# Set-up of a conditioned state-space block: evictions in front of normalisation, token loads from ScalarE's queue, a projection made in the first units

## What is computed

```
shift, scale, gate = split(silu(c) @ Wada.T + bada)
x1   = ln(x; norm1) * (1 + scale) + shift          # skip = x1
xn   = ln(x1; norm2)
mz   = xn @ Wz.T + bz ;  mx = silu(xn @ Wx.T + bx)
z1   = mz @ Wc1.T + bc1 ;  z2 = flip(mz @ Wc2.T + bc2)
y    = mx * (ssm1(z1) + flip(ssm2(z2)))
out  = x + gate * (y @ Wf.T + bf + skip)

ssm(u): dbc = u @ Wdbc.T ; dlt, B, C = split(dbc, [64, 16, 16])
        delta = softplus(dlt @ Wdt.T + bdt) ; A = -exp(Alog)
        h_t = exp(delta A) h_{t-1} + delta B u_t ;  y_t = C h_t + u_t Dp
```

## Time and profile before

| | us |
|---|---|
| median of three executions (3287.22 to 3289.47) | 3288.13 |
| the profiled execution | 3287.01 |
| its span in the profile | 3285.2 |
| the folds 2 to 15 with the last turn, 55.7 to 221.5 | 165.8 |
| from there to the main block, 221.5 to 234.4 | 12.9 |
| the main block, from 234.4 | 3050.8 |

### The profile page before, as it was taken

The page is one execution under the profiler, slowest core; times in us unless marked ns, Lnnn a source line. Parts: engine busy times, 40 slices in busy tenths (PEclk is TensorE's granted clock), DMA queues, the critical chain, the costliest instruction groups (busy, mean ns, idle before and its releaser), DMA issues.

```text
span 3285.2 us, 54883 instructions
## 1 busy us (share of the span) xinstructions
PE 2993.0 (91%) x19924; PEld 2375.2 (72%) x19924; DVE 3017.2 (92%) x2008; ACT 2678.5 (82%) x5151; POOL 2903.7 (88%) x1288
## 2 busy tenths in 40 slices
PE   8887999899998999899999999899998999899999
PEld 5765666677677666678877767678777666677789
DVE  2838999999999999999999999999998999999994
ACT  1448999988888999987788999987877999988772
POOL 1528999999999999999999999999998999999993
PEclk9989999999999999999999999999999999999999
DMA  5775334644476333645465334645566343645463
GB/s 224 236 244 171 136 117 137 227 154 163 162 248 207 130 123 131 228 144 163 159 243 192 130 123 134 224 139 165 165 217 207 120 132 130 232 136 163 156 198 111
DMA packets 207053, 560.40 MB, mean 171 GB/s; under 512 B 20200, under 2 KB 66472, under 8 KB 202560
## 3 DMA queue, kind: packets, MB, share of 16 engines
q1 hardware_dynamic: 203424, 538.01, 48.5%
q0 software_dynamic: 2304, 16.78, 1.3%
q10 hardware_dynamic: 1056, 2.10, 0.2%
HBM read 476.19 MB, written 80.63 MB: 169 GB/s over the span
## 4 chain that ended last, share of the span: by engine, by line
PE 49%; ACT 20%; DVE 12%; issue 10%; POOL 1%; DVEq 0%; ACTq 0%; POOLq 0%
PE y L888 14%; PE slot L899 10%; PE mb L859 9%; ACT abuf L1134 8%; PE mb L969 6%; DVE hbuf L1326 6%; ACT slot L1195 3%; DVE hbuf L1335 3%; PE mb L869 3%; PE slot L911 3%; DVE slot L1326 3%; ACT dec L1195 2%; PE mb L930 1%; ACT soft L1090 1%; ACT yrd L1125 1%
## 5 line engine op out<-in xcount | busy, mean ns | idle before, releaser
L1239 POOL TENSOR_TENSOR hbuf<-hbuf,cres 128x1024 f32<-128x1024 f32 x704 | 1664.4, 2377 | 143.9 <-DVE hbuf L1326 143.8
L1234 POOL TENSOR_TENSOR bst<-bst,du 128x1024 f32<-128x1024 f32 x512 | 1220.2, 2383 | 46.7 <-DVE du L1270 46.7
L1326 DVE TENSOR_TENSOR_SCAN hbuf<-dec,slot 128x1024 f32<-128x1024 f32 x512 | 1165.0, 2275 | 40.3 <-PE slot L911 27.2
L888 PE MATMUL y<-ident,hbuf 128*128 128x128 f32 x8192 | 1016.0, 273 | 1.8 <-POOL hbuf L1239 1.7
L888 PEld LDWEIGHTS y<-ident,hbuf 128*128 128x128 f32 x8192 | 923.9, 141 | 106.4 <-issue 103.5
L1134 ACT ACTIVATE abuf<-dut,bt 128x128 f32<-128x128 f32 x3072 | 964.7, 387 | 0.0
L1326 DVE TENSOR_TENSOR_SCAN slot<-slot,bst 128x1024 f32<-128x1024 f32 x320 | 728.3, 2276 | 22.5 <-ACT slot L1195 22.1
L1195 ACT ACTIVATE slot<-delta,par 128x1024 f32<-128x1024 f32 x512 | 568.4, 1110 | 199.6 <-DVE hbuf L1335 186.6
L1195 ACT ACTIVATE dec<-delta,par 128x1024 f32<-128x1024 f32 x512 | 584.2, 1141 | 118.7 <-DVE hbuf L1326 118.1
L899 PE MATMUL slot<-ident,abuf 128*128 128x128 f32 x3072 | 408.6, 276 | 170.8 <-ACT abuf L1134 160.1
L899 PEld LDWEIGHTS slot<-ident,abuf 128*128 128x128 f32 x3072 | 339.0, 141 | 303.4 <-ACT abuf L1134 243.0
(11 more groups left out here) (157 smaller groups left out, 2301.3 us busy)
## 6 DMA issues: line engine op xcount, KB each, us to landing
bst<-bc_s SPq DMA_DIRECT2D x512, 512.0 KB, 3.9
cres<-bc_s SPq DMA_DIRECT2D x128, 512.0 KB, 6.8
wzs<-wz_s SPq DMA_DIRECT2D x64, 256.0 KB, 4.0
yf_s<-yrd SPq DMA_DIRECT2D x32, 512.0 KB, 5.3
ybuf<-yf_s SPq DMA_DIRECT2D x32, 512.0 KB, 4.8
yg_s<-ybuf SPq DMA_DIRECT2D x31, 512.0 KB, 4.4
si_s<-silu SPq DMA_DIRECT2D x28, 512.0 KB, 6.1
silu<-si_s SPq DMA_DIRECT2D x28, 512.0 KB, 5.4
```

The lines of the kernel that those rows point to most:

```text
L888: last = nc.tensor.matmul(y[:, j * P:(j + 1) * P], hbuf[:, q % HR, j * P:(j + 1) * P], ident[:], start=False, stop=(q % N == N - 1), is_tr ...
L1234: nc.gpsimd.tensor_tensor(bst[:, i % BR, :], bst[:, i % BR, :], du[:, k % 2, :], ALU.mult).then_inc(pool_b, 1)
L1239: nc.gpsimd.tensor_tensor(hbuf[:, q % HR, :], hbuf[:, q % HR, :], cres[:, q % N, :], ALU.mult).then_inc(pool_prod, 1)
L1326: nc.vector.tensor_tensor_scan(h[:, ::step], decays[:, ::step], inflows[:, ::step], 0.0, ALU.mult, ALU.add).then_inc(scanned, 1)
```

## The change

1. Set-up, ScalarE: in a fold that is in both tables the turned pieces are copied out first, and the next chunk is normalised after them. The tables are as they were.
2. The loads of `xin` are issued by ScalarE: the first two in fold 1, behind a wait for the modulation weights, each other one (chunk c+2) behind the normalisation of chunk c and a wait for GpSimd's `xsk` of chunk c. GpSimd issues none and no longer waits for the normalisation before it goes to the next chunk.
3. The backward projection of chunks 0 and 1 leaves the set-up. It is dbc job 0 of the main block, made in unit 0 (c = 15) and unit 1 (c = 0) from the tokens `xn0`, copied out by ScalarE and stored in unit 1. The jobs of chunks 2 to 7 keep their units; `wproj` and its bias are loaded in unit 0 instead of unit 8.

```diff
@@ gpsimd, set-up
-            pool.wait_ge(wada_in, 32)
-            for k in range(2):
-                pool.dma_start(xin[:, k], t["x"][k]).then_inc(x_in[k], 16)
...
-                if c + 2 < NC:
-                    pool.wait_ge(n2_ready, TB * (c + 1))
-                    pool.dma_start(xin[:, k], t["x"][c + 2]).then_inc(x_in[k], 16)
@@ scalar, set-up
                     nc.scalar.activation(xn2[:, TB * c + j, :], xin[:, c % 2, j, :], ACT.Identity, scale=rs[:, 1, j:j + 1],
                                          bias=off[:, j:j + 1]).then_inc(n2_ready, 1)
+                if c + 2 < NC:
+                    act.wait_ge(n2_ready, TB * (c + 1))
+                    act.wait_ge(xsk_ready, c + 1)
+                    act.dma_start(xin[:, c % 2], t["x"][c + 2]).then_inc(x_in[c % 2], 16)
 
             for f in range(NF + 1):
+                if f in TURN_AT:
+                    transposed_tokens(TURN_AT.index(f))
                 if f in NORM_AT:
                     normalised(NORM_AT.index(f))
-                if f in TURN_AT:
-                    transposed_tokens(TURN_AT.index(f))
...
+                    if f == 1:
+                        act.wait_ge(wada_in, 32)
+                        for k in range(2):
+                            act.dma_start(xin[:, k], t["x"][k]).then_inc(x_in[k], 16)
@@ sync, vector and tensor, end of the set-up
-            for c in range(2):
-                store_projection(1, c)
...
-            sp.wait_ge(dbo_out[1], 64)
...
-            for c in range(2):
-                dve.wait_ge(dbc_mm[1], c + 1)
-                if c >= 1:
-                    dve.wait_ge(dbo_out[1], 32 * c)
-                nc.vector.tensor_scalar(dbo[:, 1, :], ps[c % 2][0:RD, :], dbias[:, 1:2], None,
-                                        ALU.add).then_inc(dbo_ready[1], 1)
...
-            pe.wait_ge(bcz_ready, NF)
-            pe.wait_ge(proj_ready[1], 2)
-            for c in range(2):
-                project(1, c, ps[c % 2])
@@ main block
-            return k - ET - 1 if ET < k < ET + 1 + NC - 2 else None
+
+            if k == 0:
+                return 0
+            return k - ET if ET < k < ET + 1 + NC - 2 else None
+
+        def dbc_part(j, i):
+
+            return (1, i) if j == 0 else (i, j + 1)
...
-                if g >= 2:
-                    sp.wait_ge(dbc_out, 128 * (g // 2))
+                if g >= 1:
+                    sp.wait_ge(dbc_out, 64 * (2 * (g // 2) + 1))
...
-                    if k == ET and c == 0:
+                    if k == 0 and c == 3:
                         sp.dma_start(wproj.rearrange("p a k r -> p (a k r)"), scratch["wproj"]).then_inc(pj_in, 16)
                         sp.dma_start(dbias, scratch["dbias"]).then_inc(pj_in, 16)
...
-            def make_dbc(j, d):
-                if d == 0:
-                    pe.wait_ge(xc_in, 16 * (j + 1))
+            def make_dbc(j, part):
+                d = dbc_part(j, part)[0]
+                tokens = xn[:, part] if j == 0 else xc
+                if part == 0:
+                    if j > 0:
+                        pe.wait_ge(xc_in, 16 * j)
                     pe.wait_ge(pj_in, 32)
```

More of the change, by code:

```diff
@@ L86, in setup_kernel @@
         xnt_mm, xnt_ready = sem("xnt_mm"), sem("xnt_ready")
-        dbc_mm, dbo_ready, proj_ready = ([sem(f"{n}{d}") for d in range(2)] for n in (
-            "dbc_mm", "dbo_ready", "proj_ready"))
-        xnt_out = sem("xnt_out")
+        dbc_mm, dbo_ready, dbo_out = (sem(n) for n in ("dbc_mm", "dbo_ready", "dbo_out"))
+        proj_ready = [sem(f"proj_ready{d}") for d in range(2)]
+        xnt_out, wproj_out = sem("xnt_out"), sem("wproj_out")
         xnt_first = [sem(f"xnt_first{c}") for c in range(2)]
-        dbo_out = [sem(f"dbo_out{j}") for j in range(2)]
         block = ctx.enter_context(nc.Block())
@@ L304, in _ @@
                     c = f - FP
-                    act.wait_ge(dbc_mm[0], c + 1)
+                    act.wait_ge(dbc_mm, c + 1)
                     if c >= 1:
-                        act.wait_ge(dbo_out[0], 32 * c)
-                    nc.scalar.activation(dbo[:, 0, :], ps[5][0:RD, :], ACT.Identity,
-                                         bias=dbias[:, 0:1]).then_inc(dbo_ready[0], 1)
+                        act.wait_ge(dbo_out, 32 * c)
+                    nc.scalar.activation(dbo[:], ps[5][0:RD, :], ACT.Identity,
+                                         bias=dbias[:, 0:1]).then_inc(dbo_ready, 1)
         @block.vector
@@ L433, in transpose_tokens, with project @@
                 last.then_inc(xnt_mm, 1)
-            def project(d, c, bank):
+            def project(c):
                 for k in range(DT):
-                    last = nc.tensor.matmul(bank[0:RD, :], wproj[:, d, k, :], xn_tile(c, k),
+                    last = nc.tensor.matmul(ps[5][0:RD, :], wproj[:, 0, k, :], xn_tile(c, k),
                                             start=(k == 0), stop=(k == DT - 1))
-                last.then_inc(dbc_mm[d], 1)
+                last.then_inc(dbc_mm, 1)
             pe.wait_ge(bz_ready, 1)
@@ L729, in store_dbc @@
             def store_dbc(j):
[L730 to L733, removed]
+                for i in range(2):
+                    d, c = dbc_part(j, i)
+                    sp.wait_ge(dbc_ready, 2 * j + i + 1)
+                    sp.dma_start(scratch["dl"][d, c], dbc[0:R, i, :]).then_inc(dbc_out, 16)
                     sp.dma_start(scratch["bc"][d, c // 2, :, c % 2 * TC:(c % 2 + 1) * TC],
-                                 dbc[R:RD, d, :]).then_inc(dbc_out, 16)
+                                 dbc[R:RD, i, :]).then_inc(dbc_out, 16)
             for n in range(3):
@@ L758, in _ @@
                         store_dbc(dbc_job(k - 1))
[L759 to L762, removed]
+                    if c == 7 and k > 0 and dbc_job(k) is not None:
+                        sp.wait_ge(dbc_mm, 2 * dbc_job(k))
+                        sp.dma_start(xc, scratch["xn"][dbc_job(k) + 1]).then_inc(xc_in, 16)
                     if c == 0 and k + 1 < NU:
@@ L955, in transpose_y @@
                     last.then_inc(ytr_mm, 1)
-            def make_dbc(j, d):
-                if d == 0:
-                    pe.wait_ge(xc_in, 16 * (j + 1))
+            def make_dbc(j, part):
[4 more added lines that the diff above has]
+                        pe.wait_ge(xc_in, 16 * j)
                     pe.wait_ge(pj_in, 32)
                 for i in range(DT):
-                    last = nc.tensor.matmul(mb[d][0:RD, :], wproj[:, d, i, :], xc[:, i, :],
+                    last = nc.tensor.matmul(mb[part][0:RD, :], wproj[:, d, i, :], tokens[:, i, :],
                                             start=(i == 0), stop=(i == DT - 1))
@@ L1159, in copy_dut, with evict_dbc @@
                 nc.scalar.activation(dut[:, half(h)], mb[h], ACT.Copy).then_inc(dut_ready, 1)
-            def evict_dbc(j, d):
-                act.wait_ge(dbc_mm, 2 * j + d + 1)
+            def evict_dbc(j, part):
+                d = dbc_part(j, part)[0]
+                act.wait_ge(dbc_mm, 2 * j + part + 1)
                 if j > 0:
                     act.wait_ge(dbc_out, 64 * j)
-                nc.scalar.activation(dbc[:, d, :], mb[d][0:RD, :], ACT.Identity,
+                nc.scalar.activation(dbc[:, part, :], mb[part][0:RD, :], ACT.Identity,
                                      bias=dbias[:, d:d + 1]).then_inc(dbc_ready, 1)
```

23 lines of the change are left out of this document (11 added, 12 removed).

## The result

The changed kernel took **3281.41 us** (median of 22 runs, 3276.20 to 3286.20), the kernel before 3287.43 (22 runs). The ratio is 0.9982, 95% interval 0.9976 to 0.9989: 5.9 us less. That is inside the range, on the side foretold and somewhat under half of the 12.7 us forecast.

What follows compares the result with a forecast made beforehand. TensorE's waits for ScalarE's copies of turned pieces were taken to bound the set-up. Loop −9.3, end of set-up −4.7 and main block +1.3 summed to −12.7, so 3275.4 us, range 3262 to 3283.

Steps and rivals of the forecast that it cites:

- What bounds the kernel: Set-up loop: TensorE waits for ScalarE's copies of turned pieces; 23.5 us lost between folds 5 and 15.
- the sum by milestones: Set-up loop: losses of folds 6, 9 and 10, less 1.0 us at fold 7, make 13.9 us to fold 12.
- Part 1: Set-up loop: copying turned pieces before normalising ends the losses of folds 6, 9, 10, 13; fold 12 13.9 us earlier.
- Part 2: Set-up: token loads from ScalarE's queue cost nothing further; 3 us is the least slack, so no wait for `off`.
- The burst: Set-up, fold 14: weights behind the main block's 4.5 MB of first loads stall TensorE nearly 10 us; loop −9.3 us.
- Part 3: End of set-up 4.7 us shorter without the backward projection; border of units 0 and 1 costs 1.3 us.
- B: Set-up loop: token loads come late from ScalarE's queue, costing 5 us, 3280.4 us; chance 0.10.
- D: Main block, units 0 and 1: moved projection not hidden, +8.3 in place of +1.3 us, 3282.4 us; chance 0.08.
- A: Set-up, fold 14: its weights are there in time, loop −21.5 us, 3263.2 us; chance 0.22.
- C: Set-up, fold 14: weights land later than the bytes say, +11 us, 3299 us; chance 0.03.
- what the profile was to show: Set-up: one 8 to 10 us weight wait before fold 14, GpSimd not waiting for normalisation, main block 14 us earlier.

Runs made afterwards that it cites:

- the order alone: Kernel before, with only ScalarE's turned pieces copied out before the next chunk is normalised; 3280.23 us, ratio 0.9981.
- the weights and the folds' stores first: Changed kernel, with SP issuing the next fold's weights and the folded tile's store ahead of the token stores; 3263.84 us, ratio 0.9923.
- the kernel with the burst last: Changed kernel, token loads back on GpSimd's queue, main block's first loads issued in SP's iteration 15 instead of 13; 3276.67 us, ratio 0.9962.

## Why the prediction was right in sign and wrong in size

**What bounds the kernel: right.** The waits for turned pieces were real and went. With the weights and the stores of the folds out of the way, fold 12 is reached 14.1 to 14.4 us earlier (89.8 − 75.7 and 89.8 − 75.4); the sum by milestones said 13.9. Folds 6 and 7 of the changed kernel took 22.1 us, the forecast's 10.9 + 10.2 + 1.0.

**Part 1, mis-sized: "To fold 12 the loop is then 13.9 us earlier".** It was 5.3. The step that failed is a missing one. I asked what is late next of the things that ScalarE and VectorE make, and of the weights only for fold 14, where a wait stood in the trace already. The other loads had little room even before. From issue to TensorE's need fold 9 had 5.7 us and fold 13 5.6; the landings took 5.6 and 6.1, and in front of fold 13 stood a wait of 0.47 us. Folds 8 and 12 had 7.5 and 7.7 us, for landings of 4.4 and 3.3. No stall lay in these stretches; what changed in the order alone is what runs beside the weights. There fold 8 landed in 7.6 us and fold 12 in 7.2, while GpSimd's queue moved 1.05 and 1.17 MB, where before it had moved 0.13 and 0.23. In the order alone that cost some 3 us (13.9 forecast, 11.1 found; waits of 1.82 and 1.21), with part 2 another 5.8.

**Part 2, "I cost it at nothing beyond the above": wrong.** By the ratios it cost some 3 us (9.2 against 5.9), which is within their intervals; by the waits, one of 4.37 us in front of fold 9 and one of 4.71 in front of fold 13 that aren't there without it, against 7.8 us less at fold 14. The forecast weighed a rule of the Trainium skill ("DMA: Bandwidth & Descriptors", section "Issuing engines are not separate DMA queues"): the moved loads free no bandwidth. The runs agree (340 and 333 GB/s). But I had the total in mind and not its division. That page of the Trainium skill says that transfers of different engines interleave; what that does to the one that somebody waits for I left out: beside GpSimd's store SP's queue had 7% of the engines' time for two microseconds, and beside the token load 32%.

**The burst: right as a mechanism.** The order alone shows 10.56 us at fold 14 against "nearly 10", and from fold 12 to fold 15 the loop lost 4.8 us against the 4.6 (13.9 − 9.3) of the sum. In the changed kernel it lost 5.1, in two waits, 4.71 and 4.22, since fold 13's own weights came late and took part of it. The two errors above, 2.8 and 5.8 us, took the loop's whole gain: −9.3 forecast, −0.15 in the profile. The clock fell behind three waits for weights, not behind one.

**Part 3: right.** End of the set-up −4.1 against −4.7; the difference is the small store, which took 6.5 us to land instead of 5.9. The border of units 0 and 1 cost 0.9 against 1.3.

**Why the time lay in the range all the same.** What is left of the change is near part 3's 4.3 us. The range ended at 3283 because B and D were allowed for, not because the loop was thought to gain nothing, so that the time falls inside is luck and doesn't speak for the sum.

**The rivals.** B's time, 3280.4, and D's, 3282.4, are equally near, but neither's mechanism came. In B's place VectorE's `st` did wait for token loads, 8.5 us in all, and ScalarE never waited for `off`. A needed the weights of fold 14 not to be held; with the weights and the folds' stores first the loop is 21.0 us shorter, A's 21.5. It needed an edit that the change doesn't make. C and D didn't come. Of what the profile was to show, four things were wrong: one wait for weights (there were four), 10.2 us between the copies of folds 6 and 7 (7.8, since fold 6's copy now comes late, behind the normalisation), the start of the main block 14 us earlier (4.0), and GpSimd free of the normalisation (it waited 22.9 us for it before its second `rs`, off the path).

The profile's span fell by 4.1 us, the medians by 6.0. The difference lies within the scatter of single executions, and the runs don't place it.

## What to carry to other kernels

When a stall goes, list every transfer that an engine needs behind it, those without a wait too: issue, landing, and the time at which the engine asks. Two loads here had 0.1 us of room or less before anything was changed. In a queue that issues loads and stores alike, put the loads that an engine waits for ahead of stores that wait for other engines; here that alone turned 6 us into 22, and on the kernel before it did nothing, so test it together with the change. A moved transfer costs no bandwidth, but it runs at another time and beside other transfers, so ask whom it will run beside.

## What the runs showed of the hardware

A load of 512 KB beside other traffic landed in 5.6 us with a 1 MB load issued a microsecond later on GpSimd's queue, and in 8.9 with the same load on ScalarE's. Where two queues were busy together they moved about as many packets each (89 and 85, 90 and 92, 116 and 121 in three stretches), so the one with the larger packets moved most of the bytes: 0.73 MB against 0.04 in two microseconds. An issue on SP is short alone (0.33 us for fold 8's weights), but behind the first loads of the main block four stores took 10.18 us to issue in the kernel with the burst last, one of them 7.70:

```profile
200.74 10.18 SPq L131 DMA_DIRECT2D xn_s<-xn  x4
```
